# Own products of a wavefront scan in three rounded passes, their parts split ahead by ScalarE and GpSimd, in a smaller arena

## What is computed

```
def step(g, inp):
    ci, ni, nm, nc = inp
    local = g[:, ci, :]
    nb = g[:, ni, :]
    neigh = (nb * nm[None, :, None]).sum(axis=1) / nc
    u = jnp.concatenate([local, neigh], axis=-1)
    y_sc = jnp.tanh(u @ w1 + b1) @ w2 + b2
    g = g.at[:, ci, :].set(local + y_sc[:, None] * w_y[None, :])
    return (g, None)
...
x = _L0_conv_ref(...)    # scan: w1 is 256 x 256, w2 256
x = _L1_conv_ref(...)    # attention with 1024 tokens, residual
x = _L2_conv_ref(...)    # attention
x = _L3_conv_ref(...)    # scan
```

## Time and profile before

| | |
|---|---|
| median of 3 runs | 4506.18 us (4506.09 to 4507.4) |
| profiled execution | 4507.79 us, its span 4505.7 us |
| first scan, levels 0 to 63 | about 43 to 542 us |
| first scan, levels 64 to 121 | to 748 us |
| attention | to about 3795 us |
| second scan | to 4505.7 us |

### The profile page before, as it was taken

The page is one execution under the profiler, slowest core; times in us unless marked ns, Lnnn a source line. Parts: engine busy times, 40 slices in busy tenths (PEclk is TensorE's granted clock), DMA queues, the critical chain, the costliest instruction groups (busy, mean ns, idle before and its releaser), DMA issues.

```text
span 4505.7 us, 56695 instructions
## 1 busy us (share of the span) xinstructions
PE 4346.3 (96%) x16776; PEld 2251.6 (50%) x16776; DVE 3472.9 (77%) x6544; ACT 2840.7 (63%) x5241; POOL 2262.9 (50%) x3972
## 2 busy tenths in 40 slices
PE   6989996999999999999999999999999999999998
PEld 2446654444444444444444444444444444445755
DVE  5988876777777777777777777777777775898877
ACT  1323322788888888888888888888888885233322
POOL 4655321455555555555555555555555556564432
PEclk9999997899999999999999999999999999999999
DMA  6668429111111122222221111111222221124211
GB/s 188 74 69 109 95 28 67 41 60 60 55 56 58 60 69 72 67 65 70 71 70 56 55 58 60 60 60 61 66 70 72 72 67 45 64 88 119 67 56 47
DMA packets 314722, 309.72 MB, mean 69 GB/s; under 512 B 253744, under 2 KB 257328, under 8 KB 309296
## 3 DMA queue, kind: packets, MB, share of 16 engines
q1 hardware_dynamic: 311312, 305.06, 27.5%
q10 hardware_dynamic: 3104, 1.06, 0.1%
HBM read 137.21 MB, written 135.27 MB: 60 GB/s over the span
## 4 chain that ended last, share of the span: by engine, by line
PE 66%; DVE 9%; ACT 8%; issue 8%; POOL 7%; DMA 1%; SPq 0%; DVEq 0%; ACTq 0%; POOLq 0%
PE psum L1179 14%; PE psum L1097 8%; PE psum L1087 6%; PE psum L1150 6%; PE psum L1111 5%; POOL probs_low L616 4%; PE psum L1163 3%; PE psum L1187 3%; PE psum L1185 3%; PE psum L1184 3%; PE psum L1222 3%; PE psum L1209 3%; PE psum L1200 3%; PE psum L1106 3%; ACT shared L992 3%
## 5 line engine op out<-in xcount | busy, mean ns | idle before, releaser
L616 POOL TENSOR_TENSOR probs_low<-shared,probs_high 128x512 fp32r<-128x512 f32 x1024 | 1307.2, 1277 | 1300.1 <-DVE probs_high L927 1300.1
L889 DVE TENSOR_REDUCE top<-psum 128x1 f32<-128x1024 f32 x1024 | 1253.9, 1225 | 616.3 <-PE psum L1163 616.0
L997 ACT ACTIVATE psum<-psum,top 128x1024 f32<-128x1024 f32 x1024 | 1114.2, 1088 | 282.0 <-DVE top L889 282.0
L992 ACT ACTIVATE shared<-psum 128x512 f32<-128x512 f32 x2048 | 1107.2, 594 | 258.9 <-PE psum L1150 258.9
L1179 PE MATMUL psum<-shared 128*128 128x512 f32 x2048 | 1123.0, 630 | 0.9 <-issue 0.5
L982 ACT ACTIVATE shared<-psum,b_col 128x320 f32<-128x320 f32 (+10 forms) x744 | 413.2, 566 | 995.9 <-PE psum L1097 981.1
L607 POOL TENSOR_TENSOR shared<-arena 128x32 f32<-128x32 f32 (+6 forms) x1230 | 584.4, 505 | 764.5 <-PE psum L1097 753.5
L1184 PE MATMUL psum<-probs_high,v_high 128*128 128x512 f32 x1024 | 811.1, 792 | 0.0
L1087 PE MATMUL psum<-arena,w_own 128*128 128x320 f32 (+12 forms) x1672 | 539.7, 450 | 35.0 <-DVE w_own L702 34.1
L1097 PE MATMUL psum<-shared,w_sum 128*128 128x320 f32 (+10 forms) x1488 | 519.5, 471 | 17.1 <-DVE shared L837 10.8
L1150 PE MATMUL psum<-q,k 64*128 64x512 f32 x2048 | 513.3, 497 | 0.3 <-ACT shared L992 0.3
(11 more groups left out here) (114 smaller groups left out, 4455.9 us busy)
## 6 DMA issues: line engine op xcount, KB each, us to landing
layer_out<-x SPq DMA_DIRECT2D x128, 512.0 KB, 2.6
x<-layer_out SPq DMA_DIRECT2D x124, 512.0 KB, 3.2
q<-q SPq DMA_DIRECT2D x256, 128.0 KB, 2.3
arena<-x_cells SPq DMA_DIRECT2D x6, 1520.0 KB, 7.0
layer_out<-arena SPq DMA_DIRECT2D x6, 1520.0 KB, 19.8
arena<-layer_out SPq DMA_DIRECT2D x6, 1520.0 KB, 10.6
y_cells<-arena SPq DMA_DIRECT2D x6, 1520.0 KB, 6.4
arena<-x_cells SPq DMA_DIRECT2D x4, 1504.0 KB, 27.9
```

The costliest lines, as they stand in the source:

```text
L616: nc.gpsimd.tensor_tensor(probs_low[n % 2][:], probs[u % PROBS], probs_high[n % 2][:], ALU.subtract).then_inc(probs_split, 1)
L889: nc.vector.reduce_max(top[i % 2][:, m:m + 1], rows_ps[m % 2][:], AX_X, negate=True).then_inc(row_max, 1)
L992: nc.scalar.activation(probs[u % PROBS], keys_ps[u % 2], ACT.Exp).then_inc(probs_ready, 1)
L997: nc.scalar.activation(rows_ps[m % 2][:], rows_ps[m % 2][:], ACT.Exp, bias=top[i % 2][:, m:m + 1], accum_out=total[i % 2][:, m:m + 1]).the ...
```

## The change

In levels 2 to 63 of both scans the own product of a stream is made in three passes with operands of type float32r, which TensorE takes in one record per matmul: high weights times high cells, low weights times high cells, high weights times low cells. "High" is the value rounded to float32r, "low" what is left of it.
- ScalarE makes the high part of the cells (`round_owns`), behind the tanh pair of the level two before; GpSimd makes the low part (`low_owns`), behind the late sums of the same level. The parts lie in the attention's tiles `k` and `q`, two buffers per stream, by the level's parity.
- TensorE's own product waits for the low part (`own_split`), and takes an ending cell among the other columns.
- VectorE makes the high and low weights in `prepare_scan`: two more instructions on 256 columns for each scan.
- To make room, chunks are at most 80 cells (96 before) and the window 400 (452): an arena of 460 cells instead of 512. There are 16 chunks instead of 14; eight are still loaded ahead, 422 cells and the ending cells instead of 483.

```diff
-CHUNK = 96
+CHUNK = 80
 TAIL = 114
-WINDOW = 452
+WINDOW = 400
...
+SPLIT_FROM = 2
...
+def in_passes_level(c, lv):
+
+    return c != BOTH and lv >= SPLIT_FROM
+
+
+def owns_done(n, lv):
+
+    return n * (JOIN - SPLIT_FROM) + lv - SPLIT_FROM + 1
...
+    own_high = [[k[2 * c + p] for p in range(2)] for c in (A, B)]
+    own_low = [[q[c][:, half(p)] for p in range(2)] for c in (A, B)]
...
+        def low_owns(n, c, lv):
+
+            if not in_passes_level(c, lv):
+                return
+            pool.wait_ge(own_rounded[c], owns_done(n, lv))
+            for o, w, place in own_parts(lv):
+                ins = nc.gpsimd.tensor_tensor(columns(own_low[c][lv % 2], c, lv, o, w), spot(c, place, w),
+                                              columns(own_high[c][lv % 2], c, lv, o, w), ALU.subtract)
+            ins.then_inc(own_split[c], 1)
...
                 for c in streams_at(lv):
                     late_sums(n, c, lv)
+                    low_owns(n, c, lv)
...
-            dve.wait_ge(scan_weights_ready, (n + 1) * (2 + HALVES))
+            nc.vector.tensor_copy(w1_high[n][:], w1_own[n][:]).then_inc(scan_weights_ready, 1)
+            dve.wait_ge(scan_weights_ready, (n + 1) * WEIGHTS_READY - 1)
+            nc.vector.tensor_tensor(w1_low[n][:], w1_own[n][:], w1_high[n][:], ALU.subtract
+                                    ).then_inc(scan_weights_ready, 1)
+            dve.wait_ge(scan_weights_ready, (n + 1) * WEIGHTS_READY)
...
+        def round_owns(n, c, lv):
+
+            if not in_passes_level(c, lv):
+                return
+            for k in first_chunks(lv, OWN_LEVEL):
+                wait_loaded(act, n, c, k, loaded, refilled, last_filled)
+            for o, w, place in own_parts(lv):
+                ins = nc.scalar.activation(columns(own_high[c][lv % 2], c, lv, o, w), spot(c, place, w), ACT.Copy)
+            ins.then_inc(own_rounded[c], 1)
...
                 squash(0, c, lv)
+                if c != BOTH and lv + 2 < JOIN:
+                    round_owns(0, c, lv + 2)
...
+            if in_passes_level(c, lv):
+                pe.wait_ge(own_split[c], owns_done(n, lv))
+                high, low = (columns(part[c][lv % 2], c, lv) for part in (own_high, own_low))
+                for h in range(HALVES):
+                    for m, (w, own) in enumerate(((w1_high, high), (w1_low, high), (w1_high, low))):
+                        nc.tensor.matmul(columns(pre(c, lv, h), c, lv), w[n][:, tile(h)], own, start=(m == 0), stop=False,
+                                         skip_group_check=True)
+                return
```

More of the change, by code:

```diff
@@ L249, in late_count @@
     return n * sum(per) + sum(per[:lv - SPAN[c].start])
+def in_passes_level(c, lv):
+    return c != BOTH and lv >= SPLIT_FROM
+def owns_done(n, lv):
+    return n * (JOIN - SPLIT_FROM) + lv - SPLIT_FROM + 1
+WEIGHTS_READY = 4 + 2
 def step_turns(c, lv):
@@ L348, in network @@
     w1_own = [sb(f"w1_own{n}", [P, HID]) for n in range(2)]
+    w1_high, w1_low = ([sb(f"w1_{part}{n}", [P, HID], F32R) for n in range(2)] for part in ("high", "low"))
     w1_sum = [sb(f"w1_sum{n}", [P, HID]) for n in range(2)]
@@ L406, in network @@
     weights_turn = sem("weights_turn")
+    own_rounded, own_split = ([sem(f"{name}{c}") for c in (A, B)] for name in ("own_rounded", "own_split"))
     weighed = [sem(f"weighed{c}") for c in (A, B)]
@@ L481, in load_first_images @@
                 sp.wait_ge(stored[A][k], 16)
-            sp.wait_ge(scan_weights_ready, 2 * (2 + HALVES))
+            sp.wait_ge(scan_weights_ready, 2 * WEIGHTS_READY)
             for i in range(DEEP):
@@ L1076, in _ @@
                 squash(1, c, lv)
+                if c != BOTH and lv + 2 < JOIN:
+                    round_owns(1, c, lv + 2)
     @block.tensor
@@ L1116, in scan @@
             own_products(n, A, 0)
-            pe.wait_ge(scan_weights_ready, n * (2 + HALVES) + 1)
+            pe.wait_ge(scan_weights_ready, n * WEIGHTS_READY + 1)
             near_products(n, A, 0)
             own_products(n, B, 0)
-            pe.wait_ge(scan_weights_ready, (n + 1) * (2 + HALVES))
+            pe.wait_ge(scan_weights_ready, (n + 1) * WEIGHTS_READY)
             for lv in range(WEIGHED):
@@ L1256, in _ @@
                 attention(j, s)
-        pe.wait_ge(scan_weights_ready, 2 * (2 + HALVES))
+        pe.wait_ge(scan_weights_ready, 2 * WEIGHTS_READY)
         pe.wait_ge(out_ready, 2 * JOBS)
```

## The result

| | before | changed |
|---|---|---|
| median | 4506.14 us (4 runs) | 4569.64 us (4 runs, 4568.07 to 4571.86) |
| span of the profiled execution | 4505.7 us | 4565.9 us |

The ratio is 1.0141, with an interval of 1.0128 to 1.0153: 63.5 us more, where 69 were forecast. That lies in the case that the prediction calls full price (4540 to 4620). The wider range of 4485 to 4640 held kernels without any loss too, so the cases and the traces say more than that range does.

A forecast was written before the change was run, and what follows sets the result against it. The prediction took a ring of near products, tanh, weighing and step product to bound the weighed levels, TensorE leading slightly in 36 to 63. 22 + 48 + 6 - 8 + 1 = +69 gave 4575 us, range 4485 to 4640.

The forecast's parts named there:

- full price: Subtraction shuts VectorE's two-input SBUF instructions out for what is left of its 1.07 us: 4540 to 4620, chance 0.62.
- Ring and side: 13-cell turn of 3.86 us: near products, tanh, weighing, step product in a ring; own products fill the hole beside it.
- TensorE's whole gain: Rival: TensorE's shorter work counts fully, 50 + 13 us gained, 4443; chance 0.04 (under 4485).
- Hidden subtraction: Rival: GpSimd gets the pair only while VectorE waits or reads PSUM; 4495, chance 0.14.
- Half price: Rival: the exclusion lasts for only part of an instruction; 4537 or less, chance 0.10.
- GpSimd the bound: Rival: GpSimd's 7.8 of 7.73 us, stretched by exclusion, holds L786; 4610 to 4650, chance 0.08.
- A slow pass: Rival: a pass takes 0.63 us, six 3.1 at 416 columns, TensorE leads; over 4700, chance 0.02.
- Levels 2 to 15: Subtraction's cost to VectorE: even targets pay 0.8, odd nothing, +0.4 average over 56 turns, 22 us.
- Levels 16 to 35: Subtraction delays VectorE's sums by 0.8 to 0.9, free 0.3 takes part: +0.6 over 80 turns, 48 us.
- Levels 36 to 63: Subtraction runs mostly beside VectorE's PSUM readers; net of TensorE's gain +0.05 over 112 turns, 6 us.
- Ending cells: Eight levels save the extra records, some 0.4 us each over 32 turns: 13 us if all count, 8 taken.
- Arena: Smaller arena: two more, smaller chunks, asked for over 60 us before they are read, cost 0.

The follow-up runs named there:

- the write: Changed kernel with own products again fp32 and the split unused, GpSimd filling a strip with zeros in place of the subtraction: 4503.52 us, ratio 0.9993.
- the runs with three lengths: Changed kernel with fp32 own products, split unused; GpSimd does the whole subtraction (4570.96 us), half its width (4528.92) or a copy instead (4513.81).
- the cells gathered alone: Kernel before, with ScalarE copying own cells side by side at the eight ending-cell levels, fp32 products: 4503.7 us, ratio 0.999.

## Why the prediction was right, and where it wasn't

- **Ring and side, right.** The own product outside the ring was the reading on which all rested, against a TensorE 96% busy; one pass instead of three leaves the turn at 3.86 us. TensorE's whole gain (4443) is out.
- **The exclusion at full price, right.** Shown by the write against the subtraction, by the three rows of level 9 and by the counts beside them. *Hidden subtraction* (4495) fell by the same; the kernel without subtraction, 4497.6, is what it would have given. *Half price* fell: each single instruction is shut out to the end. *GpSimd the bound* fell: in levels 0 to 63 of the changed kernel's first scan no instruction of VectorE waits for GpSimd, and the write, nearly as long in the queue, costs nothing. *A slow pass* fell: 0.19 apart.
- **Levels 2 to 15: 22 said, 21 measured, but not as I said.** By the earlier trace rows the sums of odd targets end at 132.27, and I let the subtraction meet VectorE's wait and update, nothing lost. I overlooked the last old sum, which starts at 132.30. In the changed kernel the same sum of the other stream takes 1.24 (at 130.77), where before it took 0.20:

```profile
128.03 0.20 DVE L786 TENSOR_TENSOR shared<-arena 128x32 f32<-128x32 f32 x1
```

  Level 9, which I had at 0, grew by 1.0 us, and level 8, where I had put the price, by 0.3. Over all fourteen levels the even ones paid 0.45 us a turn, where I had 0.8, and the odd ones 0.30, where I had 0. The average was right by luck: two errors met.
- **Levels 16 to 35: 48 and 1 for the weights said, 39 measured.** The term of 0.6 a turn was too large: 0.47. Of the 1.07 of a subtraction I let 0.47 go free (0.2 to 0.3 by its place, the rest in VectorE's 0.3 of idle time); the runs with three lengths say that some 0.6 go free.
- **Levels 36 to 63: +6 less the ending cells' half of 8 said, +6 measured.** The picture was too kind. At level 42 the subtraction runs beside the update for one stream, but for the other meets the old sums, as the timeline at ten cells shows (L871 adds the step to the sums, L1153 near product), answering to the earlier trace rows:

```profile
430.21 0.82 POOL L636 TENSOR_TENSOR q<-arena,k 128x320 fp32r<-128x320 f32 x1
...
430.46 1.45 DVE L820 TENSOR_TENSOR shared<-shared,arena 128x64 f32<-128x64 f32 x3
...
433.11 0.56 DVE L871 SCALAR_TENSOR_TENSOR shared<-psum,shared 128x288 f32<-128x288 f32 x2
...
433.73 1.34 PE L1153 MATMUL psum<-shared,w_sum 128*128 128x320 f32 x4 [0.46 <-DVE shared L871]
```

  Then VectorE's adding of the step is late and TensorE idles 0.46 us. Level 42 takes 6.94 us instead of 6.49; level 43, where it doesn't happen, 6.33.
- **Ending cells: 8 said, 3.4 measured** with the cells gathered alone. I let the eight levels count for more than half of their 13 us; the weighed ones give nothing, by the same ring.
- **Passes: 0.25 a turn said, some 0.34 measured** (1.48 less 1.14), since I took the fp32 time from a near product. It changed nothing, as the ring says.
- **Arena: 0 said, -6 measured.** I asked only whether chunks would land in time. That a product reading the arena could get shorter with its layout, and the first loads end sooner, was not in the sum. By spans the forecast was 9 us too high: 7 in levels 2 to 35 (67 said with the weights and half of the ending cells, 60 measured), 6 outside the levels of the change, and 4 the other way in levels 36 to 63 (2 said, 6 measured).
- The attention is as before: its rows are the same, and from the end of the first scan's level 63 to the second scan the changed kernel is 5 us shorter; half of that lies in the first scan's levels from 64 on and is the arena's.

## To carry over

Ask of a busy engine whether it stands in the ring: here 235 us less of TensorE's work came with 10 us, most of them the arena's, and one elementwise instruction of 0.9 us a turn on a half-idle engine cost 60. Work handed to GpSimd is paid for by VectorE when GpSimd's instruction reads SBUF and VectorE's instructions beside it have two inputs there, from the point where its length passes VectorE's slack in a turn (0.6 us here): count that slack first, and make the work a write, a shorter instruction, or ScalarE's. A wait meant to place one instruction moves all that is queued behind it.

## What the runs showed of the chip that I had not expected

- A GpSimd copy (one operand) of 480 columns takes 0.64 us against 1.21 for the subtraction, but shuts a VectorE sum with two inputs in SBUF out just as well while it lasts.
- A GpSimd write of 0.94 us beside the same sum leaves it at 0.20.
- Passes of 416 columns start 0.19 us apart: six make 1.14, against 1.42 for the four fp32 records of a near product.
- The same fp32 own product takes 1.71 us instead of 1.84 at 448 columns (seven cells of 64 images) when the arena it reads has 460 cells instead of 512 and the cells lie at other places. In all, such an arena is worth 0.1% here.
